# One stacked operand for the helical rotations: a six-block transformer step on one Trainium2 core

## The chip, the core and the metric

The kernel runs on one core of a Trainium2 chip. Its engines are TensorE (PE; PEld is its weight load), VectorE (DVE), ScalarE (ACT), GpSimd (POOL) and SyncE (SP), which here only issues transfers. Each works through its own instructions in order; they wait for each other at semaphores. The metric is the device time of one execution in microseconds (us), the median of the runs.

## What is computed

`x` is 32 sequences of 32 tokens with 128 features. Six residual blocks follow each other: cross attention with a context, an RWKV-like block, a mixture of 8 experts, a decoder layer, a helical attention, a mixture of 16 experts. The change touches the fifth only:

```python
q = x @ Wq.T + bq; k = x @ Wk.T + bk; v = x @ Wv.T + bv
qh, kh = q.reshape(b, s, h, hd), k.reshape(b, s, h, hd)      # h = 16, hd = 8
q_hel = jnp.einsum('bshd,hed->bshe', qh, Whel) + bhel        # e = 64
k_hel = jnp.einsum('bshd,hed->bshe', kh, Whel) + bhel
qn = _l2norm(q_hel.reshape(b, s, h, p, 2)).transpose(0, 2, 3, 1, 4)   # p = 32
kn = _l2norm(k_hel.reshape(b, s, h, p, 2)).transpose(0, 2, 3, 1, 4)
qn, kn = _scramble(qn), _scramble(kn)
helical = jnp.einsum('bhpsc,bhptc->bhst', qn, kn) / p
dot = jnp.einsum('bshd,bthd->bhst', qh, kh) / math.sqrt(hd)
attn = jax.nn.softmax(0.5 * dot + 0.5 * helical, axis=-1)
out = jnp.einsum('bhst,bthd->bshd', attn, vh).reshape(b, s, e)
return out @ Wo.T + bo
```

`_scramble` swaps the last two axes (tokens and the pair of components) and reads the result in the old shape, so that even and odd tokens meet in one component.

## The kernel before

Tokens lie in 8 tiles of 128, in two halves h of four tiles (512 tokens each). A half is turned to features by tokens (`YT`), and split into a part rounded to the fast matmul type and a remainder (`yTh`, `yTl`); a product at full accuracy is then three matmuls, `mm3` (lines 336 to 340): rounded with rounded, rounded with remainder, remainder with rounded.

The helical attention runs over 8 units u = (half, group g); a group has four heads. TensorE does these for a unit:

- `dots(u, w)`, for queries (w = 0) and keys (w = 1): one `mm3` of 128 rows by 512 tokens into `bank[w]`. In each group the 8 features of a head stand at the start of a strip of 32 rows (`WqD`, `WkD`), and the rest of the strip is zero. ScalarE adds the bias and writes `dot_q` (line 1041); VectorE adds it and masks even or odd strips into two copies of the keys (`mask_dot`, lines 1600 and 1601).
- `rotate(u, w, j)`: four banks `bank[2 + n % 4]` in turn. The weights `whel` are stacked by token parity, and their operands `qe_h`, `qe_l` come from `project` (line 663): a projection of the even and the odd tokens apart, once for each half and for queries and keys, biased and rounded by ScalarE (line 1027), the remainder by VectorE (`split_qk`, line 1586). For each bank and component there is first a pass that adds the bias `bhel` by a matmul against a row of ones (line 700), then an `mm3`.
- `score(u, p)`, two parts p: helical and dot scores into both banks of `pair[2]`, on 64 rows at a time. ScalarE and VectorE each `extract` half of the rows.
- `turn_weights`, `weigh_values`: the softmax weights of an earlier unit turned through `bank[0]` and weighed into `bank[1]`.

After a rotation ScalarE squares the bank (`squares`, line 1005), GpSimd adds the two components (`add_squares`, line 1188), ScalarE takes the inverse root by a logarithm and an exponential (`inverse`, lines 1010 and 1011), and VectorE multiplies (`normalise`, line 1625), which frees the bank. Operands are numbered m = 2u for queries and 2u + 1 for keys.

The order on each engine is written out in a loop over u, in which unit u is rotated while unit u - 1 is scored and unit u - 2 is weighed. The values of the second half, its projections and its turn are put between units by their number. On VectorE the bias of `bhel` is staged (`stage_bias`) in the decoder block before, out of `hbias` that SyncE loads into `wraw`; GpSimd splits `Whel`, `WqD` and `WkD` into parts after the first mixture of experts. GpSimd also splits the first pair of experts of the last block between squares (lines 1195 and 1201).

SyncE issues the loads of all inputs at the start (lines 288 to 300), then in a loop the weights of one expert at a time into `wraw` when it is free (line 311).

## Time and profile before

| what | us |
|---|---|
| median of 3 runs (lowest, highest) | 557.21 (554.51, 557.38) |
| time of the profiled execution | 557.42 |
| its span, first to last instruction | 555.6 |
| TensorE busy | 461.4 (83%) |
| VectorE busy | 414.9 (75%) |
| ScalarE busy | 299.3 (54%) |
| GpSimd busy | 99.7 (18%) |
| mean granted clock of TensorE | 0.889 of full speed |

The span is what the trace covers; 1.82 us of the execution lie around it. Busy is the time in which at least one instruction of an engine was under way. Matmuls overlap: one of 256 columns is 0.28 long, and the next starts 0.12 after it. A transfer is put down to the engine that issued it. An idle stretch in a timeline is followed by the engine and line that ended it. The granted clock is given as a share: 1.00 is 2.4 GHz, 0.50 is 1.2 GHz. A matmul of two full-accuracy operands appears as two records, so 16 of them in the program are 32 in a trace.

### The profile page before, as it was taken

What the parts mean: (1) busy time and instruction counts of PE and PEld (TensorE: products, weight loads), DVE (VectorE), ACT (ScalarE), POOL (GpSimd) and SP (SyncE); (2) the same over time, 40 slices, a digit from 0 to 9 for tenths busy, and PEclk for the clock granted to TensorE, in tenths of its full rate; (3) what the DMA queues carried; (4) which work ended last, traced back from release to release, by engine and by line L of the source; (5) the groups of instructions that cost most, each with busy time, mean ns of one, the idle gap of its engine ahead of it and who ended that gap; (6) DMA issues with size and microseconds to landing.
All of it is one profiled execution on the core that took longest, in us unless ns stands there. A gap on an engine that the chain in (4) does not pass through costs nothing.

```text
span 555.6 us, 8928 instructions
## 1 busy us (share of the span) xinstructions
PE 461.4 (83%) x2945; PEld 346.3 (62%) x2945; DVE 414.9 (75%) x1020; ACT 299.3 (54%) x565; POOL 99.7 (18%) x104
## 2 busy tenths in 40 slices
PE   5784479999999999547685979999885579999996
PEld 2342356777877777333343968888774447777774
DVE  3479867677777775767888796778767658888886
ACT  4244134566777665333233567765652227777774
POOL 1011002112221120170000121332200022222220
PEclk9978566999999999775898899999996659999999
DMA  8951000111101100000010000000001010111101
GB/s 312 408 233 57 0 1 1 57 57 58 58 4 53 57 15 2 0 1 1 1 38 1 3 1 2 2 1 2 1 2 40 0 38 1 65 48 38 38 2 38
DMA packets 7569, 24.11 MB, mean 43 GB/s; under 512 B 790, under 2 KB 3014, under 8 KB 7404
## 3 DMA queue, kind: packets, MB, share of 16 engines
q1 hardware_dynamic: 7532, 23.63, 11.6%
q8 instruction: 21, 0.34, 0.3%
q14 instruction: 16, 0.13, 0.1%
HBM read 23.11 MB, written 0.52 MB: 43 GB/s over the span
## 4 chain that ended last, share of the span: by engine, by line
PE 58%; DVE 21%; issue 8%; ACT 7%; DMA 3%; SPq 2%; POOL 1%; DVEq 0%; ACTq 0%; POOLq 0%
PE pair L338 13%; PE pair L339 13%; PE pair L340 13%; DMA arena<-in_zT 3%; PE turn L332 2%; DVE arena L1625 2%; PE pair L722 1%; PE turn L507 1%; DVE Y L1271 1%; DVE work L1447 1%; PE turn L338 1%; PE pair L648 1%; DVE st L1248 1%; PE pair L700 1%; ACT YT L846 1%
## 5 line engine op out<-in xcount | busy, mean ns | idle before, releaser
L338 PE MATMUL pair<-yTh,wh 128*128 128x512 f32 x134 | 65.5, 489 | 3.3 <-ACT work L932 3.3
L1733 DVE TENSOR_TENSOR pair<-work,turn 128x512 f32<-128x512 f32 x64 | 44.4, 696 | 18.0 <-ACT work L1097 16.3
L1097 ACT ACTIVATE work<-pair,vec 128x512 f32<-128x512 f32 x64 | 44.1, 689 | 25.5 <-PE pair L340 19.8
L339 PE MATMUL pair<-yTl,wh 128*128 128x512 f32 x134 | 55.7, 415 | 0.0
L340 PE MATMUL pair<-yTh,wl 128*128 128x512 f32 x134 | 55.3, 412 | 0.0
L1481 DVE TENSOR_TENSOR pair<-work,pair 128x512 f32<-128x512 f32 x48 | 33.3, 694 | 25.3 <-PE pair L340 22.1
L1152 POOL TENSOR_TENSOR wl<-wraw,wh 128x512 fp32r<-128x512 f32 x24 | 31.1, 1301 | 116.5 <-ACT wh L868 116.5
L932 ACT ACTIVATE work<-pair 128x512 f32<-128x512 f32 x64 | 38.3, 598 | 17.5 <-PE pair L340 16.6
L956 ACT ACTIVATE ph<-pair 128x512 fp32r<-128x512 f32 x48 | 28.7, 599 | 23.3 <-DVE pair L1481 23.1
L338 PE MATMUL pair<-ph,wh 128*128 128x512 f32 x96 | 39.1, 407 | 2.4 <-DVE pl L1501 2.3
L340 PE MATMUL pair<-ph,wl 128*128 128x512 f32 x96 | 38.4, 400 | 0.0
L339 PE MATMUL pair<-pl,wh 128*128 128x512 f32 x96 | 38.3, 399 | 0.0
L722 PE MATMUL pair<-arena 64*128 64x128 f32 x512 | 32.9, 278 | 6.3 <-ACT work L1020 4.5
L1625 DVE SCALAR_TENSOR_TENSOR arena<-work,pair 128x256 f32<-128x256 f32 x64 | 22.6, 415 | 20.2 <-ACT work L1011 20.0
L722 PEld LDWEIGHTS pair<-arena 64*128 64x128 f32 x512 | 29.9, 188 | 9.1 <-ACT work L1020 6.4
L338 PEld LDWEIGHTS pair<-yTh,wh 128*128 128x128 f32 x134 | 27.6, 206 | 10.9 <-ACT work L932 4.4
L846 ACT ACTIVATE YT<-turn 128x512 f32<-128x512 f32 x16 | 9.6, 597 | 45.4 <-PE turn L332 45.4
L1188 POOL TENSOR_TENSOR work<-work 128x512 f32<-128x512 f32 x16 | 20.4, 1280 | 74.1 <-ACT work L1005 74.1
L1501 DVE TENSOR_TENSOR pl<-pair,ph 128x512 fp32r<-128x512 f32 x48 | 32.8, 683 | 1.1 <-ACT ph L956 1.0
L340 PEld LDWEIGHTS pair<-yTh,wl 128*128 128x128 f32 x134 | 26.9, 201 | 6.8
L339 PEld LDWEIGHTS pair<-yTl,wh 128*128 128x128 f32 x134 | 27.1, 202 | 5.3
L332 PE MATMUL turn<-con,Y 128*128 128x128 f32 x56 | 12.5, 368 | 19.9 <-DVE Y L1271 13.3
(295 smaller groups left out, 1168.4 us busy)
## 6 DMA issues: line engine op xcount, KB each, us to landing
wraw<-in_w SPq DMA_DIRECT2D x8, 768.0 KB, 4.3
arena<-in_zT SPq DMA_DIRECT2D x8, 514.0 KB, 10.8
arena<-in_z SPq DMA_DIRECT2D x8, 512.0 KB, 11.5
wraw<-in_w SPq DMA_DIRECT2D x7, 512.0 KB, 3.3
mat<-in_mat SPq DMA_DIRECT2D x1, 2312.0 KB, 18.6
row<-in_row SPq DMA_DIRECT2D x1, 576.0 KB, 18.0
X<-in_x SPq DMA_DIRECT2D x1, 512.0 KB, 4.1
arena<-in_w SPq DMA_DIRECT2D x1, 512.0 KB, 3.9
```

What stands on the lines that cost most here:

```text
L338: pe.matmul(out, ah, bh, start=start, stop=False)
L339: pe.matmul(out, ah, bl, start=False, stop=False)
L340: return pe.matmul(out, al, bh, start=False, stop=stop)
L722: last = pe.matmul(pair[2][:, j, (2 * i + k) * P:(2 * i + k + 1) * P], a[rows, cols], b[rows, cols], start=n == 0, stop=n == 1, skip_group ...
L932: act.activation(act_out[q % 2], GATE0, ACT.Silu).then_inc(m["act"], 1)
L956: act.activation(ph[q % 2][:, :], UP0[q % 4], ACT.Copy).then_inc(m["hi"], 1)
L1097: act.activation(act_out[q % 2], UP1[q % 4], ACT.Relu, bias=vec[:, bass.ds(at, 1)])\
L1152: pool.tensor_tensor(wl[k][:, cols], wraw[:, cols], wh[k][:, cols].bitcast(F32), ALU.subtract)\
L1481: dve.tensor_tensor(up, act_out[q % 2], up, ALU.mult).then_inc(m["mul"], 1)
L1501: dve.tensor_tensor(pl[q % 2][:, :], UP0[q % 4], ph[q % 2][:, :].bitcast(F32), ALU.subtract)\
L1625: last = dve.scalar_tensor_tensor(out, inv, (QF, 1.0)[m % 2] * 1e12, src, ALU.min, ALU.mult)
L1733: dve.tensor_tensor(UP1[q % 4], act_out[q % 2], bank[h], ALU.mult).then_inc(m["mul"], 1)
```

## The change

The dot products and the projections are the same numbers in another arrangement, so the projections go. For each unit and w, one operand `stack(u, w)` of 128 rows is built out of the bank of the dot products. In a strip of 32 rows, rows 0 to 7 and 16 to 23 carry the rounded head features, rows 8 to 15 the remainder, rows 24 and 25 ones. This needs the query and key weights three times over in a strip (GpSimd copies them in place), and masks by row (`m_even`, `m_second` and others, in `hc`), which VectorE makes by six reductions of the identity at the start. The helical weights are laid out to match, rounded part, again, remainder and bias, by 64 small transfers of SyncE into strips, and 12 more for biases; they stand ahead of the loop that loads expert weights. The load of the parameters leaves the helical weights out. GpSimd splits the weights by the row masks.

`rotate` is then one pass: two matmuls (token parities, by a shift of the weight's columns) for each bank and component instead of four, with no bias pass. Its operands are written by `prep(u)` on ScalarE (`dot_q`, the rounded part of the query stack, even keys, the rounded part of the key stack), `stack_q(u)` on GpSimd (the query remainder) and `keys(u)` on VectorE (odd keys, the key remainder). `dot_q` and `dot_k` have three buffers instead of two. In the loop the dot products of u + 1 follow the rotations of u, the two parts of a score stand on both sides of `turn_weights`, and values of the first half stand ahead of the loop.

```diff
+        stack = lambda u, w: rslot(22 + 2 * w + u % 2)
+        by_parity = lambda v: v.rearrange("p (m c) -> p c m", c=2)
+        two_rows = lambda v: v.rearrange("p (c m) -> p c m", c=2)
...
+            sp.wait_ge(h_zero, 1)
...
+            for s in range(4):
+                for rep in range(3):
+                    r = T * s + HD * rep
+                    sp.dma_start(hc[r:r + HD, 0:8], d["vec"][T * s:T * s + HD, VEC_AT["bqD"][0]:VEC_AT["bqD"][0] + 8])\
+                        .then_inc(qk_loaded, 16)
...
             def rotate(u, w, j):
-                h, g = HEL[u]
-                n, pr = 4 * u + 2 * w + j, 2 * g + j
+
+                n = 4 * u + 2 * w + j
+                if j == 0:
+                    pe.wait_ge((h_qs, h_dk)[w], u + 1)
...
-                cols = slice((pr // 4) * 256, (pr // 4 + 1) * 256)
                 for c in range(2):
-                    bias, one = hel_bias(2 * pr + c)
-                    o = bank[2 + n % 4][:, c * 256:(c + 1) * 256]
-                    pe.matmul(o, bias, one, start=True, stop=False)
-                    last = mm3(o, whel(wh, 2 * pr + c), whel(wl, 2 * pr + c), qe_h(h, w)[:, cols], qe_l(h, w)[:, cols],
-                               False, True)
+                    for par in range(2):
+                        last = pe.matmul(bank[2 + n % 4][:, c * 256:(c + 1) * 256], whel(4 * (u % 4) + 2 * j + c, par),
+                                         stack(u, w)[:, par * 256:(par + 1) * 256], start=par == 0, stop=par == 1)
                 last.then_inc(h_hel, 1)
...
+            def prep(u):
+                g = u % 4
+                act.wait_ge(h_d, 2 * u + 1)
+                if u >= 3:
+                    act.wait_ge(h_s, 2 * u - 4)
+                act.activation(dot_q(u), bank[0], ACT.Identity, bias=q_bias(g))
+                act.activation(two_rows(stack(u, 0)), by_parity(bank[0]), ACT.Identity, bias=q_bias_lo(g), scale=m_second)\
+                    .then_inc(h_dq, 1)
+                act.wait_ge(h_d, 2 * u + 2)
+                act.activation(dot_k(u, 0), bank[1], ACT.Identity, bias=k_bias_even(g), scale=m_even)
+                act.activation(two_rows(stack(u, 1)), by_parity(bank[1]), ACT.Identity, bias=k_bias_lo(g), scale=m_second)\
+                    .then_inc(h_hk, 1)
 
             inverse_std(0)
             copy_turned(yt(0))
-            for w in range(2):
-                project(0, w, bank[6 + w])
             round_turned(0)
+            act.wait_ge(h_w, 1)
+            prep(0)
             inverse_std(1)
...
+            def stack_q(u):
+                pool.wait_ge(h_dq, u + 1)
+                s = two_rows(stack(u, 0))
+                pool.tensor_tensor(s, by_parity(dot_q(u)), s.bitcast(F32), ALU.subtract).then_inc(h_qs, 1)
...
+            def keys(u):
+                dve.wait_ge(h_hk, u + 1)
+                if u >= 3:
+                    dve.wait_ge(h_s, 2 * u - 4)
+                dve.tensor_scalar(dot_k(u, 1), bank[1], k_bias(u % 4), m_odd, ALU.add, ALU.mult)
+                s = two_rows(stack(u, 1))
+                dve.scalar_tensor_tensor(s, by_parity(bank[1]), k_bias(u % 4), s.bitcast(F32), ALU.add, ALU.subtract)\
+                    .then_inc(h_dk, 1)
```

Three places where the order moves. First VectorE at the start of the stage, behind the norm of the second half's decoder result, before the change (line 1600 and 1601 are `mask_dot`, 1625 `normalise`, 1633 the value blocks):

```order
L1579 TENSOR_TENSOR X<-Y2b,X 128x512
L1248 BN_STATS st<-X 128x6 x4
L1251 BN_AGGR mv<-st 128x2 x4
L1600 TENSOR_SCALAR arena<-turn,vec,con 128x512
L1601 TENSOR_SCALAR arena<-turn,vec,con 128x512
L1625 SCALAR_TENSOR_TENSOR arena<-work,pair 128x16x16 x8
L1633 TENSOR_TENSOR Y2b<-pair,con 128x4x32 x4
```

And the same place after it (1610 and 1612 are `keys`, 1645 the value blocks, 1637 `normalise`):

```order
L1599 TENSOR_TENSOR X<-Y2b,X 128x512
L1273 BN_STATS st<-X 128x6 x4
L1276 BN_AGGR mv<-st 128x2 x4
L1610 TENSOR_SCALAR arena<-turn,hc 128x512
L1612 SCALAR_TENSOR_TENSOR arena_r<-turn,hc,arena_r 128x512
L1645 TENSOR_TENSOR Y2b<-pair,con 128x4x32 x4
L1645 TENSOR_TENSOR wraw<-pair,con 128x4x32 x4
L1645 TENSOR_TENSOR arena<-pair,con 128x4x32 x8
L1610 TENSOR_SCALAR arena<-turn,hc 128x512
L1612 SCALAR_TENSOR_TENSOR arena_r<-turn,hc,arena_r 128x512
L1637 SCALAR_TENSOR_TENSOR arena<-work,pair 128x16x16 x8
```

The keys of unit 0 stand where `mask_dot` stood, behind the norm, but a rotation now waits for them; the value blocks and the keys of unit 1 moved ahead of `normalise`.

Next ScalarE in unit 3, before (1041 writes `dot_q`, 1047 is the exponential, 1005 the squares, 1010 and 1011 an inversion, 1060 the copy of the turned weights, 1020 an extraction):

```order
L1041 ACTIVATE arena<-turn,vec 128x512
L1047 ACTIVATE work<-work 128x512
L1005 ACTIVATE work<-pair 128x512 x4
L1010 ACTIVATE work<-work,lntiny 128x512
L1011 ACTIVATE work<-work,cq 128x512
L1060 ACTIVATE work<-turn 128x512
L1010 ACTIVATE work<-work,lntiny 128x512
L1011 ACTIVATE work<-work,ck 128x512
L1020 ACTIVATE work<-pair 32x2x2x64 x2
```

And in the same unit after (1035 to 1040 are `prep` of the next unit, 1027 the extractions):

```order
L1012 ACTIVATE work<-pair 128x512 x4
L1058 ACTIVATE work<-work 128x512
L1035 ACTIVATE arena<-turn,hc 128x512
L1036 ACTIVATE arena_r<-turn,hc 128x512
L1039 ACTIVATE arena<-turn,hc 128x512
L1040 ACTIVATE arena_r<-turn,hc 128x512
L1017 ACTIVATE work<-work,lntiny 128x512
L1018 ACTIVATE work<-work,cq 128x512
L1027 ACTIVATE work<-pair 32x2x2x64 x2
L1069 ACTIVATE work<-turn 128x512
L1017 ACTIVATE work<-work,lntiny 128x512
L1018 ACTIVATE work<-work,ck 128x512
```

Three activations came in, squares stand ahead of the exponential, and an extraction stands between the two inversions.

Last TensorE between two units, after the change (768 is `weigh_values`, 717 the rotations, 364 to 366 the dot products of the next unit, 738 and 743 a score):

```order
L768 MATMUL turn<-Y2b,work 128x128
L768 MATMUL turn<-wraw,work 128x128
L768 MATMUL turn<-arena,work 128x128 x2
L717 MATMUL pair<-arena_r,wh 128x256 x16
L364 MATMUL turn<-yTh,xch 128x512
L365 MATMUL turn<-yTl,xch 128x512
L366 MATMUL turn<-yTh,xcl 128x512
L364 MATMUL turn<-yTh,xch 128x512
L365 MATMUL turn<-yTl,xch 128x512
L366 MATMUL turn<-yTh,xcl 128x512
L738 MATMUL pair<-arena 128x128 x2
L743 MATMUL pair<-arena 128x128 x2
```

Before, the dot products of a unit (338 to 340) stood ahead of its own rotations, and a half score ahead of them:

```order
L749 MATMUL turn<-arena,work 128x128 x2
L722 MATMUL pair<-arena 128x128 x16
L338 MATMUL turn<-yTh,xch 128x512
L339 MATMUL turn<-yTl,xch 128x512
L340 MATMUL turn<-yTh,xcl 128x512
L338 MATMUL turn<-yTh,xch 128x512
L339 MATMUL turn<-yTl,xch 128x512
L340 MATMUL turn<-yTh,xcl 128x512
L700 MATMUL pair<-pl,ph 128x256
L338 MATMUL pair<-arena_r,wh 128x256
L339 MATMUL pair<-arena_r,wh 128x256
L340 MATMUL pair<-arena_r,wl 128x256
```

The last four rows stand eight times there in a unit, 32 matmuls, against 16 now; the second half of a score moved ahead of the weighing.

## Rows read from the trace of the kernel before

**Rows 1.** Timelines of TensorE: start, length, engine, line, instruction, count, idle before it

```profile
344.44 0.28 PE L700 MATMUL pair<-pl,ph 128*128 128x256 f32 x1
...
355.65 0.50 PE L338 MATMUL turn<-yTh,xch 128*128 128x512 f32 x1
...
357.40 0.28 PE L700 MATMUL pair<-pl,ph 128*128 128x256 f32 x1
...
361.17 0.60 PE L734 MATMUL turn<-con,work 128*128 128x128 f32 x4
...
361.70 2.06 PE L722 MATMUL pair<-arena 64*128 64x128 f32 x32
...
365.39 0.49 PE L749 MATMUL turn<-Y2b,work 128*128 128x128 f32 x2
...
366.48 0.71 PE L722 MATMUL pair<-arena 64*128 64x128 f32 x8
...
398.86 0.28 PE L700 MATMUL pair<-pl,ph 128*128 128x256 f32 x1
...
424.10 1.11 PE L332 MATMUL turn<-con,Y 128*128 128x128 f32 x4 [2.01 <-DVE Y L1665]
```

**Rows 2.** Windows: stretch, length, busy time (records) by engine, clock, DMA share, GB/s

```profile
306.00:314.00 8.00, 8.00 (x60) 7.31 (x61) 6.01 (x18) 2.85 (x5) 1.29 (x1) 0.68 0.00 0
...
406.00:418.00 12.00, 8.33 (x113) 7.34 (x111) 9.57 (x23) 4.88 (x11) 0.00 (x0) 1.00 0.00 1
```

**Rows 3.** Timelines of the start of the stage, ScalarE, TensorE, VectorE

```profile
299.24 0.60 ACT L846 ACTIVATE YT<-turn 128x512 f32<-128x512 f32 x1 [2.55 <-PE turn L332]
...
303.57 0.63 ACT L860 ACTIVATE yTh<-YT 128x512 fp32r<-128x512 f32 x1
...
305.60 0.16 DVE L1266 TENSOR_TENSOR rt<-ry 128x4 f32<-128x4 f32 x1
...
305.83 0.77 PE L338 MATMUL turn<-yTh,xch 128*128 128x512 f32 x1 [3.03 <-POOL yTl L1145]
...
307.48 0.69 ACT L1041 ACTIVATE arena<-turn,vec 128x512 f32<-128x512 f32 x1 [2.86 <-PE turn L340]
...
310.42 0.38 DVE L1251 BATCH_NORM_AGGREGATE mv<-st 128x2 f32<-128x6 f32 x4
```

**Rows 4.** Timeline of ScalarE in a middle unit

```profile
359.38 1.71 ACT L1005 ACTIVATE work<-pair 128x512 f32<-128x512 f32 x3
...
361.86 0.71 ACT L1010 ACTIVATE work<-work,lntiny 128x512 f32<-128x512 f32 x1
```

**Rows 5.** Timeline of VectorE in a middle unit

```profile
363.36 1.41 DVE L1625 SCALAR_TENSOR_TENSOR arena<-work,pair 128x256 f32<-128x256 f32 x4 [2.12 <-ACT work L1011]
364.70 0.84 DVE L1610 COPY work<-pair 32x256 f32<-32x256 f32 x2
...
366.90 0.87 DVE L1633 TENSOR_TENSOR Y2b<-turn,con 128x128 f32<-128x128 f32 x4
...
368.48 1.18 DVE L1660 TENSOR_TENSOR Y<-turn,hstat 32x128 f32<-32x128 f32 x4
...
371.29 0.69 DVE L1643 TENSOR_TENSOR work<-work,hstat 128x512 f32<-128x512 f32 x1
372.02 0.81 DVE L1600 TENSOR_SCALAR arena<-turn,vec,con 128x512 f32<-128x512 f32 x1
```

**Rows 6.** Timelines of GpSimd and VectorE, behind the stage

```profile
430.20 1.27 POOL L1145 TENSOR_TENSOR yTl<-YT,yTh 128x512 fp32r<-128x512 f32 x1 [25.42 <-ACT yTh L860]
...
430.70 0.79 DVE L1266 TENSOR_TENSOR rt<-ry 128x4 f32<-128x4 f32 x1 [0.47 <-ACT ry L854]
```

**Rows 7.** Timelines of SyncE's issues (SPq) and of ScalarE

```profile
18.96 1.08 SPq L300 DMA_DIRECT2D mb<-in_mb  x1
...
199.51 0.27 SPq L305 DMA_DIRECT2D wraw<-in_hbias  x1
...
43.97 72.18 SPq L311 DMA_DIRECT2D wraw<-in_w  x3
...
88.99 0.62 ACT L868 ACTIVATE wh<-wraw 128x512 fp32r<-128x512 f32 x1
```

More of the change, by code:

```diff
@@ L655, in _ @@
                 last.then_inc(f_out, 1)
-            def project(h, w, b):
-                parity = yt(h).rearrange("p (m c) -> p c m", c=2)
-                for g in range(2):
-                    for c in range(2):
-                        last = pe.matmul(b[64 * c:64 * c + 64, g * 256:(g + 1) * 256],
-                                         mcol(("WqE", "WkE")[w], g * 64, 64), parity[:, c, :], start=True, stop=True)
-                last.then_inc(h_e, 1)
             def dots(u, w):
@@ L775, in _ @@
             n = turn4(lambda i: Y[:, i, :])
+            pe.wait_ge(h_w, 1)
+            for w in range(2):
+                dots(0, w)
             pe.wait_ge(feat_ready, n)
-            for w in range(2):
-                project(0, w, bank[6 + w])
-            pe.wait_ge(h_w, 1)
-            pe.wait_ge(h_bias, 1)
+            for t in range(HT):
+                values(t, blk(bank[6], t))
             for u in range(len(HEL) + 2):
-                if u % 4 == 0 and u < len(HEL):
-                    pe.wait_ge(y_lo, 2 + u // 4)
-                    pe.wait_ge(h_ec, 2 + u // 2)
@@ L785, in _ @@
                 if u < len(HEL):
                     for w in range(2):
-                        dots(u, w)
-                    for w in range(2):
-                        if u == 2 and w == 1:
-                            pe.wait_ge(h_dk, 3)
-                            turn4(lambda i: Y[:, HT + i, :])
                         for j in range(2):
                             rotate(u, w, j)
-                if u == 0:
-                    for t in range(HT):
-                        values(t, blk(bank[6], t))
@@ L797, in _ @@
-                if u >= 2 and u != 8:
+                if u + 1 < len(HEL):
+                    for w in range(2):
+                        dots(u + 1, w)
+                if u == 7:
+                    project_out(0)
+                if 1 <= u <= len(HEL):
+                    score(u - 1, 0)
+                if u >= 2:
                     turn_weights(u - 2)
                 if 1 <= u <= len(HEL):
-                    score(u - 1, 0)
-                if u == 8:
-                    turn_weights(6)
-                    score(7, 1)
@@ L814, in _ @@
+                if u in (4, 5):
+                    pe.wait_ge(h_dq, u + 2)
+                    pe.wait_ge(h_ets, u - 1)
+                    for t in (2 * (u - 4), 2 * (u - 4) + 1):
+                        values(HT + t, blk(bank[0], t))
                 if u == 6:
@@ L1204, in _ @@
             y_rest(0, 3)
+            stack_q(0)
             for m in range(2 * len(HEL)):
                 add_squares(m)
-                if m == 6:
+                if m % 2 == 1 and m // 2 + 1 < len(HEL):
+                    stack_q(m // 2 + 1)
+                if m == 3:
                     y_rest(1, 4)
@@ L1671, in add_out @@
                 dve.tensor_tensor(half(X, h), bank[1], half(X, h), ALU.add).then_inc(h_x, 1)
-            dve.wait_ge(h_bias, 1)
+            dve.wait_ge(h_w, 1)
+            keys(0)
+            for t in range(HT):
+                value_blocks(t, blk(bank[6], t))
             for u in range(len(HEL) + 2):
-                if u < len(HEL):
-                    mask_dot(u)
                 if u == 8:
```

250 lines of the change are left out of this document (115 added, 135 removed).

## Prediction

> **What bounds the kernel now.** I read the windows first, to find the stretch that the change touches, and then the timelines of one unit in it, engine by engine. The helical attention runs from about 299 us, when the normalised tokens have been turned, to 424.10 us, when the second half of its result is turned [rows 1]; all that follows waits for that turn and is not edited. There are eight units u, two query/key operands each. From unit 3 to unit 7 the first rotation matmul moves from 344.44 to 398.86 us [rows 1], 54.4 us for four units, 13.6 each. In one such unit TensorE works without a pause: dot products at 355.65, rotations from 357.40, the turned weights at 361.17, half a score at 361.70, weighing at 365.39, the other half at 366.48 [rows 1]. The clock is at full speed there and stays so even in 406 to 418 us, where TensorE is busy for 8.33 of 12 us [rows 2]. So TensorE is the bound of the middle units: what is taken from it comes back, but only until another engine's chain is longer. That chain is the question of this case.
>
> **TensorE's part of the change.** A rotation of one unit is 32 matmuls of 256 columns from 357.40 to 361.17, 3.77 us or 0.118 each [rows 1]. The change leaves 16, 1.9 us, so 8 x 1.9 = 15 us less in all. The four projections and their splits go too. If TensorE stayed the bound, that alone would give 15 us, and I use it as the far end of a gain. Scores (2.06), weighing (366.48 - 365.39 = 1.09), turned weights (0.53) and dot products (six at 0.23, 1.4 without the wait in between) [rows 1] are kept, so TensorE needs 1.9 + 1.4 + 0.5 + 4.1 + 1.1 = 9.0 us a unit and can no longer set a period of 13.6.
>
> **ScalarE's part.** Per unit it loses nothing in the middle and gains three activations of 512 columns: both `stack` writes and the even keys. `prep` is four such, priced by the one that exists, 0.69 [rows 3], pitch about 0.67, so 2.7 us. I find no row of a read by parity from a bank; the nearest rows are plain activations at 0.57 to 0.69 [rows 3, 4]. From above I bound it by twice that, 1.4 us more a unit; from below by nothing, since a permuted read moves the same elements. I take the plain price, since the element count is what the 0.57 and 0.69 rows share.
>
> The four squares cost 2.28 (three in 1.71), an inversion 1.44 (two of 0.71), an extraction 0.8, the exponential and the copy of turned weights 0.57 each [rows 4]. Sum for a unit: 2.28 + 0.55 + 2.7 + 2.88 + 1.6 + 0.58 = 10.6 us.
>
> **The loop that becomes the bound.** The order of the change ties ScalarE and TensorE: the rotations start, 0.72 later the first square (four matmuls of 0.118 and a handover of 0.25), squares 2.28, exponential 0.55, prep 2.7, inversion 1.44, extraction of the first half of the scores 0.8; only then may TensorE write the second half (0.1 + 2.06), weigh (1.14 with its wait) and rotate the next unit. 0.72 + 2.28 + 0.55 + 2.7 + 1.44 + 0.8 + 0.1 + 2.06 + 1.14 = 11.8 us. Units 4 and 5 also compute values between these, from 363.8 to 365.39, 1.5 us [rows 1]: 13.3. Unit 6 turns results, 0.6: 12.4.
>
> VectorE has a loop of its own: normalise 1.34, extraction 0.87, shift (0.69 + 0.73 with its start), result 1.22, then the dot products may overwrite the bank (0.15 + 0.69), score 2.06, extraction 0.87, keys 1.5 (two like the 0.81 row), normalise 1.34 [rows 5]: 11.5 us, with the value blocks (two times four of 0.87 with overlap, 1.6) 13.1. It is just under the other. So the four units take 11.8 + 13.3 + 13.3 + 12.4 = 50.8 us where they took 54.4: 3.6 us gained.
>
> **The start of the stage.** Now the dot products stand ahead of everything: the copy of the turned tokens ends at 299.84, the rounding that stood at 303.57 can follow at once, and the dot products follow it by 2.26 as now [rows 3], so at 302.15 instead of 305.83. But ScalarE takes the statistics of the other half only after prep(0): first bank 1.65 after the start of the dot products [rows 3], 303.8, four activations to 306.5, the inverse at 307.1 where it is used at 305.60 now. VectorE's norm behind it takes 5.2 us (305.60 to the end of 310.42) [rows 3], to 312.3, and keys(0) stands behind that, with the rotation of the keys waiting for it: 313.9 us. Four value blocks follow (3.2), then keys(1) at 318.9, normalise 320.4 to 323.1; TensorE rotates unit 1 from 321.2. By the same prices: score of unit 0 at 325.1, prep(2) to 327.3, inversion, extraction to 329.5, second half to 331.7, the turn of the other half, its copy and rounding to 333.7, then a loop of 11.1 to the rotation of unit 3 at 344.8. That is 0.4 later than the 344.44 of now: the early start is eaten up.
>
> And TensorE then stands still from about 310 to 313.9 and from 316.3 to 321.2. The clock was at 0.68 on average in 306 to 314 us, behind a stretch with little work [rows 2]; I expect half speed again for the pieces around 314 to 326: 0.4 us for four rotation matmuls, 1.25 for dot products, up to the next prep and score 2.3 us in all. So the rotation of unit 3 starts between 344.8 and 347.1; I take 346.0.
>
> **The end of the stage.** From the rotation of unit 7 to the last turn it is 424.10 - 398.86 = 25.2 us [rows 1]. Rotations lose 1.9, and the output projection of the first half, which now stands ahead of the score, adds 0.9: 24.15. Sum: 346.0 + 50.8 + 24.15 = 420.95, so 3.15 us earlier than 424.10.
>
> **Parts with one answer.** The bias staging on VectorE ran under the decoder's second product, and the norm behind it waits for ScalarE's activations of the other half: nothing. The six mask reductions stand where VectorE waits for the first cross attention: nothing, and six instructions of the 0.16 to 0.4 kind if that cover were gone. GpSimd's preparation of the weights keeps its size and ends 50 us ahead of its use. `stack_q`, a subtraction of 1.27 us like the one in [rows 6], runs under the inversions; 8 of them lie beside other work.
>
> **SyncE.** 76 small transfers stand ahead of the load of the second expert's weights, which is issued at 43.97 now and first used at 88.99 [rows 7]. An issue cost 1.08 at 18.96 us and 0.27 at 199.51 [rows 7]. Starting at 20.0 the last is issued at 40.5 at the least and at 102 at the most. I take about 0.4, since the bulk loads that slow the early ones end by 35 us: some 50 us, well ahead of 89. The Trainium skill ("SBUF — State Buffer", The DMA setup-cost knee) says that every transfer has a roughly fixed 2 us, mostly completion. Taken one after another that would be 152 us and the load would come at 172, some 85 us late; but this trace issues 1.08 apart or less with many in flight, so it is latency and the trace does not bear the serial reading out.
>
> **Rivals.** (1) *The clean case*: the handovers between ScalarE and TensorE hide and only ScalarE's own 10.6 counts: 1.2 less in each of four units, 1.2 at the start: 9 us earlier, 548. For it: the loop is only 1.2 us above ScalarE's sum. (2) *A lock between VectorE and GpSimd*. A product of 128x4 on VectorE, 0.16 long at 305.60 [rows 3], took 0.79 us at 430.70 and ended with a GpSimd subtraction that had begun at 430.20 and lasted 1.27 [rows 6]. In the new order the squares come ahead of the exponential, so GpSimd's sum of squares lands where VectorE subtracts the maximum (two operands from SBUF); if GpSimd is first, VectorE's loop grows from 11.5 to as much as 12.8 us and passes 11.8. With 1.0 us in each of five units: 559. It decides from GpSimd starting less than 1.9 us after the rotation; by my times it starts at 1.95 and VectorE is 0.3 ahead. The Trainium skill ("SBUF — State Buffer", Who interferes with whom) says that a VectorE instruction with two SBUF inputs and a GpSimd one that reads SBUF exclude each other for the whole instruction; the row agrees. (3) *The clock falls in the middle units*: TensorE works 9.0 of 12.7 us, with waits of about 1.3 and 1.9 us. At half speed its 9.0 become 18 and it is the bound again; with half of the units so, 10 us more than forecast: 565, slower. Against it: 8.33 of 12 us busy kept full speed [rows 2]. [...] (4) *The issues on SyncE cost 1.08 each*: expert 2's weights land at about 106 instead of before 89, 17 us late: 575. (5) *The gain isn't there, reads by parity cost double*: 1.4 us a unit on ScalarE's loop, six units: 562.
>
> **How the numbers follow.** The profiled execution took 557.42 us with a span of 555.6, the median is 557.21. 557.21 - 3.15 = 554.1. Chances: forecast 0.42 (its own range 552 to 556), clean 0.15, lock 0.18, clock 0.14, SyncE 0.05, parity reads 0.06. About 0.5% (2.8 us, so 554.4) is what a measurement of this kernel can tell from no change. Faster: 0.15 and 0.27 of the forecast; same: 0.15 of the forecast, the lock and a little of the clock case, 0.34; slower 0.24. The range leaves out the full 15 us of TensorE below, and SyncE and half of the clock case above: 547.5 to 563.
>
> **What would show it.** Rotation pieces of 16 matmuls in 1.9 us; ScalarE's four activations per unit at 0.6 to 0.7; a distance between rotations of 11.8 us at unit 3 and 13.3 at units 4 and 5; ScalarE busy for nine tenths of it; the first rotation of keys at about 314; a VectorE subtraction of more than 1 us for the lock; a granted clock below 1.00 between 330 and 400 us for the clock case. I am wrong if the middle units take less than 11 us, or if the stage starts late by more than the 2.3 us.

## The result and the profile after

| | median, us | runs |
|---|---|---|
| before | 556.27 (553.86 to 558.51) | 11 |
| after | 560.97 (557.76 to 565.19) | 11 |

The ratio is 1.0086, with a 95% interval of 1.0061 to 1.0111: slower by 0.9%, some 4.7 us, where 3.15 us less was forecast. The profiled execution of the changed kernel took 558.86 us, span 557.0, and is the second shortest of its eleven. The ratios here and below leave out runs more than 1.5% above the fastest of their kernel, which are two of twelve in the first experiment and three of six in the one with more work for TensorE.

The busy times, from the page of the changed kernel:

```profile
PE 446.4 (80%) x2785; PEld 332.7 (60%) x2785; DVE 412.8 (74%) x1013; ACT 310.9 (56%) x581; POOL 117.3 (21%) x114
```

TensorE lost 15 us of work, as computed from the rotations, and the mean clock fell from 0.889 to 0.873. The table shows where the span went. Its borders are turns (TensorE's transposes, L332 before and L358 after) and the first rotations of units 3 and 7 (L700, L717). The last two columns are experiments told below. Each column is one profiled execution, and that of the three edits (543.75 us) is the shortest of its six:

| stretch of the span, us | before | after | three edits | four edits |
|---|---|---|---|---|
| to the router's turn | 74.43 | 75.36 | 72.13 | 72.17 |
| first experts | 160.06 | 158.33 | 158.43 | 158.85 |
| decoder's self attention | 15.12 | 17.63 | 14.13 | 14.14 |
| rest of the decoder | 48.94 | 49.03 | 49.42 | 49.90 |
| helical stage to rotation 3 | 45.89 | 47.11 | 41.71 | 43.47 |
| rotation 3 to rotation 7 | 54.42 | 52.76 | 52.64 | 50.73 |
| rotation 7 to the last turn | 25.24 | 25.89 | 23.33 | 24.03 |
| last experts | 131.5 | 130.9 | 130.1 | 130.9 |

The first two lines can't be put down to the change: nothing of TensorE's order was edited there, and the first of them is 71.9 to 75.6 us in the eleven kernels traced with the new order, on both sides of the 74.43 of before. They move with the clock (granted 0.51 to 0.80 between 25 and 40 us in the changed kernel's trace, 1.00 in that with three edits).

**One middle unit after.** Timeline of TensorE from rotation 3 to rotation 4 (start, length, engine, line, instruction, count, idle before it), which answers to [rows 1]:

```profile
347.46 2.14 PE L717 MATMUL pair<-arena_r,wl 128*128 128x256 f32 x16
349.44 0.39 PE L364 MATMUL turn<-yTh,xch 128*128 128x512 f32 x1
...
351.50 0.47 PE L364 MATMUL turn<-yTh,xch 128*128 128x512 f32 x1 [1.21 <-DVE Y L1672]
...
354.36 0.66 PE L755 MATMUL turn<-con,work 128*128 128x128 f32 x4
356.13 0.49 PE L738 MATMUL pair<-arena 64*128 64x128 f32 x4 [1.11 <-ACT work L1027]
...
359.02 2.13 PE L717 MATMUL pair<-arena_r,wh 128*128 128x256 f32 x16
```

The 16 matmuls take 2.0 us until the next work, the unit 11.56 us, and there are two waits now where before had none: for VectorE's result of an older unit, and for ScalarE's extraction. ScalarE in the same unit, which answers to [rows 4]:

```profile
348.28 2.07 ACT L1012 ACTIVATE work<-pair 128x512 f32<-128x512 f32 x4 [0.85 <-PE pair L717]
350.20 0.65 ACT L1058 ACTIVATE work<-work 128x512 f32<-128x512 f32 x1
350.72 0.71 ACT L1035 ACTIVATE arena<-turn,hc 128x512 f32<-128x512 f32 x1
351.29 0.81 ACT L1036 ACTIVATE arena_r<-turn,hc 128x512 fp32r<-128x512 f32 x1
352.48 0.78 ACT L1039 ACTIVATE arena<-turn,hc 128x512 f32<-128x512 f32 x1 [0.37 <-PE turn L366]
353.16 0.77 ACT L1040 ACTIVATE arena_r<-turn,hc 128x512 fp32r<-128x512 f32 x1
353.82 0.72 ACT L1017 ACTIVATE work<-work,lntiny 128x512 f32<-128x512 f32 x1
```

A plain read (L1035, L1039) is followed by the next instruction after 0.57 and 0.68 us, a read by parity (L1040) after 0.66. Windows of units 3 to 6 (length, busy time and records by engine, clock, DMA share, GB/s), beside [rows 2]:

```profile
347.46:359.02 11.56, 9.23 (x101) 7.90 (x100) 9.18 (x23) 10.03 (x18) 4.87 (x4) 1.00 0.00 0
359.02:372.05 13.03, 10.70 (x166) 9.32 (x164) 10.48 (x29) 10.03 (x18) 6.10 (x5) 1.00 0.01 3
372.05:387.13 15.08, 12.28 (x166) 10.71 (x164) 11.13 (x30) 10.14 (x18) 5.45 (x4) 0.89 0.01 2
387.13:400.22 13.09, 9.64 (x106) 8.30 (x104) 12.01 (x31) 10.55 (x19) 4.67 (x3) 1.00 0.01 1
```

Units 3 and 4 come at 11.6 and 13.0 us, as computed. Unit 5 takes 15.1, and its clock is 0.89.

**The self attention, 60 us ahead of the stage.** Timelines of VectorE, then GpSimd, after:

```profile
244.46 0.84 DVE L1289 TENSOR_SCALAR ve<-mv 128x4 f32<-128x4 f32 x1
245.33 1.24 DVE L1291 TENSOR_TENSOR rt<-ry 128x4 f32<-128x4 f32 x1
246.60 1.01 DVE L1292 SCALAR_TENSOR_TENSOR rt<-rt,ve 128x4 f32<-128x4 f32 x1
247.65 1.01 DVE L1293 SCALAR_TENSOR_TENSOR ry<-rt,ry 128x4 f32<-128x4 f32 x1
```

```profile
234.97 3.94 POOL L1186 TENSOR_SCALAR wh<-mat,hc 128x1440 fp32r<-128x1440 f32 x1
...
242.54 2.73 POOL L1195 TENSOR_TENSOR wh<-mat,wh 128x1440 fp32r<-128x1440 f32 x1
245.23 1.32 POOL L1195 TENSOR_TENSOR wl<-mat,wl 128x640 fp32r<-128x640 f32 x1
246.50 2.13 POOL L1197 TENSOR_TENSOR xcl<-mat,xch 128x512 fp32r<-128x512 f32 x2
```

Four instructions on 128x4 take 4.1 us together, and each ends within 0.04 us of the end of a GpSimd subtraction: 245.30 by 245.27, 246.57 by 246.55, 247.61 and 248.66 by the middle and the end of the pair of L1197 (246.50 to 248.63). Elsewhere in this trace the same four lines take 0.16 or 0.17 each, but for one of 0.69 and one of 0.78. It is the effect of [rows 6], four times in a row. In the kernel before the same subtractions ended earlier, and only two of the four were met (VectorE):

```profile
244.93 0.60 DVE L1264 TENSOR_SCALAR ve<-mv 128x4 f32<-128x4 f32 x1
245.56 1.00 DVE L1266 TENSOR_TENSOR rt<-ry 128x4 f32<-128x4 f32 x1
246.60 0.16 DVE L1267 SCALAR_TENSOR_TENSOR rt<-rt,ve 128x4 f32<-128x4 f32 x1
```

The Trainium skill ("SBUF — State Buffer", Who interferes with whom) calls the port pair that VectorE and GpSimd share an exclusive lock; these rows agree, with 0.16 us of work taking 0.84 to 1.24.

### The profile page after: what moved, and what is told of

Same layout as the page of the kernel before. It is cut to its first block, busy times and chain, and to the rows that moved or that the text cites. A ratio compares the mean times of both kernels' runs of the same rounds, so it can differ in the third digit from the quotient of the medians.

```text
span 557.0 us, 8713 instructions
## 1 busy us (share of the span) xinstructions
PE 446.4 (80%) x2785; PEld 332.7 (60%) x2785; DVE 412.8 (74%) x1013; ACT 310.9 (56%) x581; POOL 117.3 (21%) x114
## 4 chain that ended last, share of the span: by engine, by line
PE 55%; DVE 26%; ACT 8%; issue 6%; DMA 3%; SPq 2%; POOL 0%; DVEq 0%; ACTq 0%
PE pair L364 12%; PE pair L366 12%; PE pair L365 12%; DMA arena<-in_zT 3%; DVE arena L1637 2%; PE turn L358 2%; PE pair L738 2%; PE turn L533 1%; DVE Y L1672 1%; DVE work L1622 1%; PE pair L743 1%; DVE st L1273 1%; DVE work L1479 1%; PE pair L674 1%; PE turn L364 1%
## 5 line engine op out<-in xcount | busy, mean ns | idle before, releaser
L366 PE MATMUL pair<-yTh,wl 128*128 128x512 f32 x134 | 54.8, 409 | 0.0
L738 PE MATMUL pair<-arena 64*128 64x128 f32 x256 | 28.2, 295 | 10.6 <-ACT work L1027 7.9
L1210 POOL TENSOR_TENSOR work<-work 128x512 f32<-128x512 f32 x16 | 22.2, 1396 | 50.8 <-ACT work L1012 50.8
L738 PEld LDWEIGHTS pair<-arena 64*128 64x128 f32 x256 | 21.1, 197 | 15.1 <-ACT work L1027 11.4
L1153 POOL TENSOR_TENSOR yTl<-YT,yTh 128x512 fp32r<-128x512 f32 x4 | 5.1, 1268 | 110.6 <-ACT yTh L867 110.6
L358 PE MATMUL turn<-con,Y 128*128 128x128 f32 x56 | 13.7, 396 | 16.4 <-DVE Y L1296 12.7
## 6 DMA issues: line engine op xcount, KB each, us to landing
mat<-in_mat SPq DMA_DIRECT2D x1, 520.0 KB, 14.9
```

What stands on the lines that cost most here:

```text
L358: last = pe.transpose(blk(bank[n % 2], i), src(i), ident)
L366: return pe.matmul(out, al, bh, start=False, stop=stop)
L738: pe.matmul(o, rot(4 * u + k)[rows, cols], rot(4 * u + 2 + k)[rows, cols], start=True, stop=False, skip_group_check=True)
```

## Three losses, each taken away alone, and together

The theory after reading the two traces is that the loop of a unit is as computed, and that three things around it cost more than the loop gives: GpSimd's longer work in the self attention, the output projection of the first half in the tail, and ScalarE's order at the start. The rival is that these are waits that something else covers, and the time went into TensorE's lower clock.

**GpSimd's work early.** The buffers of the helical weights are free when expert 6 is done, and GpSimd is idle then:

```diff
-            pool.wait_ge(moe[0]["down"], SUMMED[0][1])
-            pool.wait_ge(tok_ready, 8)
+            pool.wait_ge(moe[0]["down"], 2 * NF0 * (NE0 - 1) + FREE0["down"])
             pool.memset(wl[0][:, 5 * P:5 * P + T].bitcast(F32), 0.0)
...
+            pool.wait_ge(moe[0]["down"], SUMMED[0][1])
+            pool.wait_ge(tok_ready, 8)
             strips = [(xch[0][:, :], xcl[0][:, :], mcol("WqD")), (xch[1][:, :], xcl[1][:, :], mcol("WkD"))]
```

> GpSimd's rounding and remainder of the rotation weights moves from behind the first expert layer into its last expert, where GpSimd is idle; only the small strips stay behind the layer. Theory A (the second cross attention pays for GpSimd holding VectorE): in the changed kernel three 128x4 products took 1.24, 1.01 and 1.01 us where 0.16 is usual; they return to at most 0.2 to 1.0, the distance from the turn at 233.69 to the one at 251.32 (17.63 us) falls to 15.5 or less, and the whole runs about 2 us faster than the changed kernel, so 1.005 of the kernel before. Theory B (the loss is the granted clock, spread over the program): the products shrink, but the time stays within 0.5 us of the changed kernel's, 1.008.

Measured: 556.77 us, ratio 1.0007 (0.9973 to 1.0041), so 0.8% or 4.4 us less than the change as it was; by the two intervals that is 2 to 7 us. VectorE in the self attention of this run:

```profile
240.48 0.17 DVE L1291 TENSOR_SCALAR ve<-mv 128x4 f32<-128x4 f32 x1
241.12 0.16 DVE L1293 TENSOR_TENSOR rt<-ry 128x4 f32<-128x4 f32 x1 [0.47 <-ACT ry L861]
241.32 0.16 DVE L1294 SCALAR_TENSOR_TENSOR rt<-rt,ve 128x4 f32<-128x4 f32 x1
```

The stretch fell from 17.63 to 13.22 us here. In the seven later kernels with this edit on top of others it was 14.13 to 14.16, in the two experiments without it (the next two) it was 17.63 both times. So 3.5 us go with GpSimd's work: 3.0 are the hold of the four instructions above, once the wait of 0.47 that comes back is counted, and 0.5 an earlier one on 128x4, which took 0.65 instead of 0.17 beside GpSimd's multiplications. The rest of this run's gain there is a faster clock (0.83 to 1.00 where the changed kernel has 0.50). Theory A holds, and I had put the price too low.

**The output projection late.**

```diff
-                if u == 7:
-                    project_out(0)
                 if 1 <= u <= len(HEL):
                     score(u - 1, 0)
+                if u == 7:
+                    project_out(0)
```

> The output projection of the first half stands behind the first half of the score of unit 6 instead of ahead of it. Theory A (it holds that score, since it waits for the result of unit 4 on VectorE): the score follows the rotation of unit 7 within 0.3 us instead of 2.6, and the distance from that rotation to the last turn falls from 25.9 to about 24.0, 1.9 us less: 1.005 of before. Theory B (the loop behind it is bound elsewhere, by the softmax of unit 6 on VectorE and ScalarE): the score comes earlier, but the last turn less than 0.5 us earlier: 1.008.

Measured: 558.98 us, ratio 1.0052 (1.0023 to 1.0081), 1.9 us less. That interval overlaps the one of the change as it was (1.0061 to 1.0111), so the time alone does not show the gain; the trace does. TensorE behind rotation 7, first after, then in this run:

```profile
400.22 2.13 PE L717 MATMUL pair<-arena_r,wl 128*128 128x256 f32 x16
403.78 1.16 PE L791 MATMUL turn<-mat,work 128*128 128x128 f32 x8 [1.43 <-DVE Y L1672]
404.87 0.49 PE L738 MATMUL pair<-arena 64*128 64x128 f32 x4
```

```profile
403.00 2.14 PE L717 MATMUL pair<-arena_r,wl 128*128 128x256 f32 x16
405.07 0.49 PE L738 MATMUL pair<-arena 64*128 64x128 f32 x4
```

The score starts 2.07 behind the rotation instead of 4.65, and rotation 7 to the last turn falls from 25.89 to 24.44. Over the traces of the changed order that stretch is 25.9 to 28.4 us in three without this edit and 23.3 to 25.2 in six with it; in the last two experiments, which change more of the order, it is 24.3 and 26.8. This is what theory A said.

**The statistics first.**

```diff
+            inverse_std(1)
             act.wait_ge(h_w, 1)
             prep(0)
-            inverse_std(1)
```

> ScalarE takes the statistics of the second half ahead of its four activations for unit 0 instead of behind them. Theory A (VectorE's norm of the second half, held by ScalarE's order, is the start's wait): VectorE's product follows its statistics at 304.4 instead of 308.72, the first key rotation moves from 315.33 to 311.1, and the rotation of unit 3 from 347.5 to 343.5: 4 us faster than the changed kernel, 1.001 of before. Theory B (TensorE's clock at half speed in the start sets the time, or GpSimd's sum of squares): the rotation of unit 1 comes less than 2 us earlier, 1.005.

Measured: 554.7 us, ratio 0.999 (0.9967 to 1.0013), 5.3 us less. VectorE, after and in this run (L1610 is the first of `keys(0)`):

```profile
302.98 0.69 DVE L1289 TENSOR_SCALAR ve<-mv 128x4 f32<-128x4 f32 x1
308.72 0.16 DVE L1291 TENSOR_TENSOR rt<-ry 128x4 f32<-128x4 f32 x1 [5.05 <-ACT ry L861]
...
313.84 0.78 DVE L1610 TENSOR_SCALAR arena<-turn,hc 128x512 f32<-128x512 f32 x1
```

```profile
298.72 0.69 DVE L1289 TENSOR_SCALAR ve<-mv 128x4 f32<-128x4 f32 x1
299.44 0.16 DVE L1291 TENSOR_TENSOR rt<-ry 128x4 f32<-128x4 f32 x1
...
304.57 0.78 DVE L1610 TENSOR_SCALAR arena<-turn,hc 128x512 f32<-128x512 f32 x1
```

From the statistics to the first keys it is 10.9 us after and 5.9 here. From the turn that opens the stage (300.35 and 296.10) rotation 3 comes after 47.11 and 42.91 us. Theory A holds.

**The three together.**

> The three edits together: GpSimd's rounding early, the output projection late, the statistics first. Theory A: the three losses stand behind one another and add, 2 + 1.9 + 4 = 8 us less than the changed kernel: 0.994 of before. Theory B (clock): the saved waits come back as a lower clock, under half of it, 1.001 or more.

Measured: 547.48 us, ratio 0.9862 (0.9825 to 0.9899), 2.2% or 12.5 us less than the change as it was; the three alone sum to 11.6, which is the same within the intervals. So the three losses stood behind one another, and the clock took nothing back on the whole. The rival falls as the main cause. The result, 547.5, is what the clean case of the prediction gave, 548, though for another reason.

**Is it the change or the edit?** The same early rounding in the kernel before:

> The kernel before with GpSimd's rounding and remainder of the largest rotation weight moved into the last expert, as in the first of these experiments: what that edit is worth without the change. Theory A (GpSimd holds VectorE in the second cross attention in both kernels, 1.00 and 0.60 us where 0.16 is usual in the one before): the distance from the turn at 234.49 to that at 249.61 falls from 15.1 to 14.1 or less, and the time by 1 us or more: 0.998. Theory B (only the changed kernel's longer GpSimd work reaches that norm): unchanged within 0.5 us, 1.000.

Measured: 553.85 us, ratio 0.9971 (0.9951 to 0.9991). The stretch fell from 15.12 to 14.04. So 1.1 of the 3.5 us was there before; the change itself had added 2.4, and with its three losses removed it is still 1.1% faster than the kernel before with the same edit.

## Which loop sets the period

**The rotations twice over**, on top of the three edits:

```diff
-                for c in range(2):
+                for c in (0, 0, 1, 1):
```

> The three edits, and each rotation matmul pair is done twice, which puts the 1.9 us a unit back that the change took from TensorE; nothing else is changed. Theory A (the loop of a unit runs through rotation, squares, exponential, the four activations, inversion, extraction, score and weighing): the second pass delays the last square by 1.6 to 1.9 us, so a unit of 11.6 becomes 13.2 to 13.5, and eight units cost 13 us: 1.009 of before; less whatever TensorE's clock gives back since it is busier. Theory B (a loop of VectorE sets the period and TensorE has room): less than 0.7 us a unit, 0.995 or less.

Measured: 1.0077 (1.0049 to 1.0106), 2.15% or 12 us more than without it. Units 3 and 6 take 12.88 and 13.26, units 4 and 5 15.9 and 15.6 with a clock of 0.89. An added microsecond of rotation thus costs 0.8 us over the whole: TensorE is in the loop. The forecast's path, through the last square that waits for the last bank, fits with it, though this run does not single it out. The cost is not equal in all units: unit 3 grew by 1.3 us, unit 6 by 0.2 (13.09 with the three edits). There VectorE's subtraction was held by GpSimd for 0.39 us with the three edits and is not in this run; against the 12.2 of that unit without a hold (next section) it is 1.0.

**One activation twice**, also on top of the three:

```diff
+                step(act.activation(dot_q(u), bank[0], ACT.Identity, bias=q_bias(g)))
                 act.activation(dot_q(u), bank[0], ACT.Identity, bias=q_bias(g))
```

> The three edits, and in every unit the first of ScalarE's four activations is done twice, one behind the other: 0.7 to 0.75 us more of ScalarE a unit and nothing else. Theory A (ScalarE's four activations stand in the loop of TensorE and ScalarE): every unit gets longer by all of it, 11.55 to 12.3 where the clock holds, 5 us in all: 0.995 of before. Theory B (VectorE's loop is as long, or TensorE's waits hide it): less than 0.3 us a unit, 0.989 or less.

Measured: 0.9954 (0.9927 to 0.9981), 0.92% or 5.1 us more, for 5 us expected. Unit 3 took 13.44 for the 12.3 that was expected, with a fall of the clock in it; unit 6 took 13.30, only 0.2 more than with the three edits. Over the whole, what is added to ScalarE comes out at the end as what is added to TensorE does, so both are in the loop; in unit 6, where VectorE's subtraction is held (next section), the added work is mostly hidden.

## The clock in the middle units

The granted clock in steps of 1 us in unit 5, after (columns as in the windows above):

```profile
376.00:377.00 1.00, 0.00 (x0) 0.00 (x0) 0.96 (x4) 1.00 (x2) 1.00 (x2) 1.00 0.00 0
377.00:378.00 1.00, 0.76 (x3) 0.48 (x3) 0.93 (x3) 0.78 (x2) 1.00 (x1) 0.89 0.00 0
378.00:379.00 1.00, 1.00 (x7) 0.68 (x8) 0.10 (x1) 0.57 (x1) 1.00 (x2) 0.50 0.00 0
...
381.00:382.00 1.00, 1.00 (x15) 0.88 (x12) 0.21 (x1) 0.46 (x2) 0.00 (x0) 0.90 0.00 0
```

TensorE had waited, and what held it was VectorE (TensorE, then VectorE):

```profile
377.24 0.47 PE L364 MATMUL turn<-yTh,xch 128*128 128x512 f32 x1 [2.35 <-DVE Y L1672]
```

```profile
371.24 0.88 DVE L1645 TENSOR_TENSOR Y2b<-turn,con 128x128 f32<-128x128 f32 x4 [0.17 <-PE turn L777]
...
374.42 1.45 DVE L1655 TENSOR_TENSOR work<-work,hstat 128x512 f32<-128x512 f32 x1
375.90 1.19 DVE L1672 TENSOR_TENSOR Y<-turn,hstat 32x128 f32<-32x128 f32 x4
```

The value blocks push the subtraction of the maximum (L1655) into GpSimd's sum of squares (374.04 to 375.33), so it takes 1.45 instead of 0.69, and the second dot product waits for the result behind it. Then the clock is at 1.2 GHz for some 3.4 us. The kernel before has no fall between rotations 3 and 7. The profiled execution after has one; those of the first two experiments, whose order there is the same, have three and two. The hold and the fall can be priced apart, because the traces have units with neither, with the hold alone and with both. The first column is from the fourth edit, told below, which moves the subtraction ahead of the value blocks:

| us | neither | hold | hold and fall |
|---|---|---|---|
| unit 5 | 13.31, four edits | 14.17, statistics first | 15.08, after |
| unit 6 | 12.23, four edits | 13.09, after | 14.00, the first two experiments |

A hold with the wait behind it costs 0.9 us, and a fall another 0.9. Unit 3 shows how little decides about a hold. It took 11.56 us after and 13.23 in the first experiment, where nothing was edited in it. GpSimd, then VectorE, after:

```profile
349.44 1.82 POOL L1210 TENSOR_TENSOR work<-work 128x512 f32<-128x512 f32 x1 [7.04 <-ACT work L1012]
349.45 0.69 DVE L1655 TENSOR_TENSOR work<-work,hstat 128x512 f32<-128x512 f32 x1
```

The same two in the experiment with GpSimd's work early:

```profile
343.65 1.28 POOL L1212 TENSOR_TENSOR work<-work 128x512 f32<-128x512 f32 x1 [7.03 <-ACT work L1012]
343.66 1.83 DVE L1657 TENSOR_TENSOR work<-work,hstat 128x512 f32<-128x512 f32 x1
```

Both start within 0.01 us of each other; one time GpSimd is held, the other time VectorE, and there a wait of 2.35 and a fall of the clock follow. In the kernel before the subtraction takes 0.69 in all eight units.

The changed kernel scatters more (557.76 to 565.19, where before has 553.86 to 558.51), and its median is 3.3 us further from the median of before than one profile is from the other. Holds and falls that come in some executions and not in others would do both, but this is not shown: one execution of each kernel was traced, and the mean granted clock does not put its eleven runs in order (0.873 at 558.86 us, 0.883 at 563.42, 0.863 at 565.19).

**The subtraction ahead of the value blocks**, as a fourth edit:

```diff
+                if 1 <= u <= len(HEL):
+                    extract(u - 1, 1)
+                    softmax_shift(u - 1)
                 if u in (4, 5):
                     for t in (2 * (u - 4), 2 * (u - 4) + 1):
                         value_blocks(HT + t, blk(bank[0], t))
-                if 1 <= u <= len(HEL):
-                    extract(u - 1, 1)
-                    softmax_shift(u - 1)
```

> The three edits and a fourth: in units 4 and 5 VectorE takes the second half of the scores and subtracts the maximum ahead of the value blocks. With the three edits the units that start at 347.4 and 360.4 take 13.0 and 15.0 us. Theory A (the subtraction meets GpSimd's sum of squares there, 1.45 for 0.69 us, and the exponential and the second dot product wait for it): the subtraction falls to 0.7 and both units get shorter by 0.8 to 1.0 us each, 0.9828 of before after 0.9862. Theory B (the first dot product needs the value blocks out of its bank, so the wait only moves there): unchanged within 0.5 us.

Measured: 546.97 us, ratio 0.9852 (0.9816 to 0.9887). In the trace it does what theory A says: the subtraction takes 0.69, the waits ahead of the second dot product that were 2.34 are gone (0.9 of each moved ahead of the first dot product, which waits for the value blocks, as theory B has it), and units 5 and 6 take 13.3 and 12.2 us instead of 15.0 (with a fall) and 13.1. But unit 3 had a fall in this execution (12.5 instead of 11.55), and 0.9852 cannot be told from 0.9862. As a gain in time it stays unproved.

**More work for TensorE**, on top of the three edits:

```diff
-                for i in range(HT):
-                    last = pe.transpose(blk(bank[0], i), blk(ex(u), i), ident)
+                for i in range(HT * 3):
+                    last = pe.transpose(blk(bank[0], i % HT), blk(ex(u), i % HT), ident)
```

> The three edits, and the turn of the weights is written three times over in every unit, into the same bank, where TensorE otherwise waits 1.1 us for ScalarE: extra work without any use. Theory A (TensorE has so many waits now that its granted clock falls in the middle units, 0.87 to 0.89 in one or several of them, at 1.2 to 2 us each): the clock stays at 1.00 through the middle units and the whole gets 1 to 3 us faster in spite of more work, 0.983. Theory B (the falls come from elsewhere or cost nothing): the clock still falls in the middle units, time unchanged or up to 2 us longer, 0.986 to 0.990.

Measured: 0.9883 (0.9829 to 0.9937), no gain. Its six runs took 546.16 to 555.14 us; the ratio is that of the three shorter ones, and the traced one is the longest. In this trace TensorE was busy 85% of units 4 and 5 (13.06 of 15.40 us in unit 4) and the clock fell there and in unit 6. The double rotations above show the same: 13.93 of 15.91 us busy in unit 4, and a fall. So theory A as I had put it falls. Each of the three falls here came at or behind the end of a wait of 2.34 for VectorE's result, which the filler had not touched; it had filled the other wait. So I put it again: the falls stand behind single long waits, whatever the busy share around them.

**Another order, with and without the filler**, on top of the four edits:

```diff
                 if u + 1 < len(HEL):
-                    for w in range(2):
-                        dots(u + 1, w)
+                    dots(u + 1, 0)
                 if 1 <= u <= len(HEL):
                     score(u - 1, 0)
+                if u + 1 < len(HEL):
+                    dots(u + 1, 1)
...
                     .then_inc(h_dq, 1)
+                between()
                 act.wait_ge(h_d, 2 * u + 2)
...
                 if u + 1 < len(HEL):
-                    prep(u + 1)
+                    prep(u + 1, lambda: inverse(2 * u))
...
```

> The four edits, and another order on two engines: TensorE does the first half of the score between the two dot products, ScalarE does the first inversion between the query and the key activations. Theory A (the waits for the result of the unit before, ahead of the second dot product, and for the extraction are on the loop): a unit without values takes 11.0 instead of 11.6 us and the wait ahead of the second dot product, 1.2 to 2.3 us, is gone, and with it some of the falls of the clock: 2 to 5 us less, 0.977 to 0.982 of before. Theory B (the keys on VectorE, now 1 us later, or the longer wait behind the turn of the weights take it back): 0.984 to 0.988.

> The same, with the turn of the weights written three times over into the same bank, work without any use, in the wait that this order puts behind it. Theory A (every fall of the clock in the middle units follows a TensorE wait of 1.9 us or more by about 1 us; shorter waits are not followed by one): the longest wait there falls to about 1.2, the clock holds 1.00 from unit 3 to unit 7, 1 to 3 us less than without the filler: 0.973 to 0.980. Theory B (falls come at other waits too, as in the filler run before): the same as without it, or up to 1 us more.

Measured: 0.9901 (0.9864 to 0.9939) without the filler and 0.9883 (0.9844 to 0.9922) with it: neither is better than the three edits. On the clock the two traces are clear. Between rotations 3 and 7, without the filler TensorE waits 2.04 to 2.72 behind the turn of the weights and the clock fell in all four units; with it no wait is over 1.86, and the clock held. Windows of unit 4 in the first and in the second:

```profile
352.16:366.19 14.03, 11.97 (x166) 10.76 (x164) 10.87 (x27) 9.95 (x18) 5.56 (x5) 0.88 0.01 2
```

```profile
351.47:364.01 12.54, 11.36 (x173) 10.25 (x172) 10.62 (x27) 9.95 (x18) 6.11 (x5) 1.00 0.01 3
```

These four units take 54.8 us in the first trace and 50.8 in the second, but the executions are as long as each other (549.65 and 549.81), and the medians 550.44 and 549.61 are not told apart: a held clock there has not been shown to shorten the whole. The gain of 0.5 us a unit that the new order was to bring went elsewhere: the keys of the next unit come later on VectorE, so the first two units take 9.3 and 13.5 us where they took 7.9 and 12.2 with the four edits, and in the second of these runs the tail took 26.8 instead of 24.0, at a clock of 0.87. No version beyond the three or four edits is shown to be better.

## Why the prediction was wrong, point by point

- **TensorE's part, right.** 15 us less work; a rotation takes 2.0 us for 1.9.
- **ScalarE's part and the loop, right.** Four activations at 0.57 to 0.68; units of 11.56 and 13.03 for 11.8 and 13.3; ScalarE busy 10.03 of 11.56. A read by parity costs no more than another, so rival 5 falls.
- **The start of the stage, right.** From the first turn to rotation 3: 47.45 forecast, 47.11 measured. The first key rotation came 15.0 us behind that turn for 15.35. The statistics behind `prep(0)` were in that sum, but I took the wait as given: that order alone is 4 to 5 us of the change's time.
- **SyncE, right.** The 76th issue ended at 50.1 us for "some 50", and the expert weights were used at 88.91 for 88.99 before [rows 7]. The reading of one transfer after another at 2 us falls with it.
- **"GpSimd's preparation of the weights keeps its size and ends 50 us ahead of its use", the step that failed first.** It took 14.9 us instead of 12.0 (233.76 to 248.63 after, 234.56 to 246.55 before), and its deadline was not what mattered: it lay beside a norm of VectorE whose small instructions it holds. The stretch grew by 2.5 us, and the sum has no term for it. I had the price in [rows 6] and looked for the hold only inside the stage.
- **Units 5 and 6, mis-sized.** 50.8 forecast for rotations 3 to 7, 52.76 measured. Unit 5 took 15.1 where 13.3 was meant, unit 6 13.1 where 12.4 was. The subtraction is held in both (by 0.76 and 0.39 us), and unit 5 has a fall of the clock as well. With the fourth edit, which moves the subtraction and leaves neither, they took 13.3 and 12.2, so the loop had the right size. The step that failed is the margin of rival 2, "VectorE is 0.3 ahead": GpSimd and VectorE started within 0.01 us of each other in units 3 and 4, and in units 5 and 6 GpSimd was 0.38 and 0.75 ahead.
- **The tail, mis-sized.** 24.15 forecast, 25.89 measured. "The output projection ... adds 0.9" counted its length; it also waits 1.43 for a result of VectorE, and the score behind it waits too. The forecast is itself 0.1 short: 25.24 - 1.9 + 0.9 is 24.24.
- **The sum.** At the last turn the profile is 2.0 us late where I had 3.15 early: +1.8 up to the start of the stage (of which 2.5 in the self attention, and -0.7 in what lies ahead of and behind it), -0.3 to rotation 3, +2.0 to rotation 7, +1.7 to the last turn. Behind that turn it gained 0.6. The other 3.3 us between the two medians are in neither trace, and their cause stays open.
- **The clock, rival 3, true in part.** It had 0.14 and a price of 10 us at half of the time at half speed. It came as one fall of some 3.4 us in unit 5, at a price of 0.9, with TensorE busy for 12.28 of 15.08 us (81%), above the 8.33 of 12 us that I had taken as proof against it [rows 2]. The share was the wrong thing to read: the longest wait tells more.
- **A rival's price.** The 575 of rival 4 does not follow: 17 us on top of the forecast is 571.

The range held the median (560.97), but the sign was wrong: the step in the self attention had no term, the tail was too short, and two rivals on the slow side came true at the same time, in small.

## What to carry to other kernels

When work is moved onto GpSimd or grows there, look at what VectorE does at that time, not only at when the result is due: a row of tiny instructions can be held for the length of each GpSimd one. When an engine gets work, go through every instruction that is now queued behind it, an unrelated norm included, and price the wait. Where a GpSimd and a VectorE instruction start within 0.01 us of each other, which of them is held can change from one trace to the next; a hold of VectorE was worth 0.9 us here. And when TensorE's work shrinks, look for the longest wait that is left in a unit: a fall of the clock may stand behind it.

## What the runs showed of the hardware

- In the thirteen kernels traced, each of the 20 falls of the clock between rotations 3 and 7 lasted 3.0 to 4.0 us, read in steps of 0.5, and began between 0.4 us ahead of the end of a TensorE wait of 1.9 to 2.7 us and 1.7 us behind it. There are 32 such waits, so 12 were not followed by one (2.34 at 390 us after was not). Waits up to 1.86 were not followed by any. What decides between two equal waits was not found.
- A VectorE subtraction of 128x512 with both operands in SBUF takes 0.69 us, and 1.45 (374.42 after) or 1.83 (343.66 in the first experiment) beside a GpSimd sum of 1.28 to 1.29. GpSimd's own sum takes 1.82 where it is the one that is held (349.44 after).
- GpSimd's multiplication by a per-row scalar took 3.94 us for 1440 columns, 2.7 ns a column; its subtraction of the same columns 2.73, 1.9 ns a column.
